# A decoder layer with eight experts: weight chunks rounded first, one tile's products in three parts, scores turned four tiles at a time

## The reference, cut to what matters

```python
x = layernorm(x + attention(x))                     # causal, 16 heads of 128
x = layernorm(x + cross_attention(x, ctx))          # linear attention, gated, 16 heads of 32
x = layernorm(x + ffn(x))

def ffn(h):                                          # h: 896 tokens x 512
    logits = h @ router_weight.T + router_bias       # 8 experts
    top_vals, top_idx = top_k(logits, 2)
    scores = zeros_like(logits).at[rows, top_idx].set(softmax(top_vals))
    gate_up = einsum('th,ehj->etj', h, gate_up_proj) + gate_up_proj_bias
    gate, up = minimum(gate_up[..., ::2], 7), clip(gate_up[..., 1::2], -7, 7)
    act = (up + 1) * gate * sigmoid(1.702 * gate)
    expert_out = einsum('eti,eih->eth', act, down_proj) + down_proj_bias
    return einsum('te,eth->th', scores, expert_out)
```

## Time and profile before

| what | value |
|---|---|
| median of 3 runs | 908.39 us (906.37 to 908.43) |
| the profiled execution | 907.49 us, span 905.7 us |
| PE busy (matmul) | 836.1 us, 92% of the span |
| DVE, ACT, POOL busy | 468.6, 309.7, 103.6 us |
| mean granted clock of PE | 0.964 |
| chain that ended last | PE 71%, no visible wait ("issue") 9%, DVE 8%, ACT 7% |

### The profile page before, as it was taken

The page is one execution under the profiler, slowest core; times in us unless marked ns, Lnnn a source line. Parts: engine busy times, 40 slices in busy tenths (PEclk is TensorE's granted clock), DMA queues, the critical chain, the costliest instruction groups (busy, mean ns, idle before and its releaser), DMA issues.

```text
span 905.7 us, 12521 instructions
## 1 busy us (share of the span) xinstructions
PE 836.1 (92%) x4878; PEld 731.5 (81%) x4878; DVE 468.6 (52%) x867; ACT 309.7 (34%) x705; POOL 103.6 (11%) x95
## 2 busy tenths in 40 slices
PE   7999999999999999899999999999778999999970
PEld 6998997989898989788898788888557787888760
DVE  4445454544536462758622443556756666656424
ACT  4533333232424342532432121222223454444420
POOL 0000000000000000000000001102301323443342
PEclk9999999999999999999999999999859999999995
DMA  9680817240202012022100111102763546654325
GB/s 331 242 280 6 284 38 233 89 160 32 96 1 87 13 25 98 6 85 91 35 1 1 35 35 58 46 13 96 290 201 120 178 144 168 179 132 107 73 35 182
DMA packets 35903, 97.92 MB, mean 108 GB/s; under 512 B 6649, under 2 KB 9081, under 8 KB 33153
## 3 DMA queue, kind: packets, MB, share of 16 engines
q1 hardware_dynamic: 32032, 88.62, 28.5%
q0 software_dynamic: 3808, 8.46, 5.1%
HBM read 64.03 MB, written 32.12 MB: 106 GB/s over the span
## 4 chain that ended last, share of the span: by engine, by line
PE 71%; issue 9%; DVE 8%; ACT 7%; DMA 2%; POOL 2%; POOLq 0%; SPq 0%; ACTq 0%; DVEq 0%
PE bank L306 57%; PE bank L655 3%; ACT w_gu L1031 3%; PE bank L687 2%; PE bank L584 2%; POOL y_acc L511 1%; DVE hh L1833 1%; PE bank L643 1%; DVE prob L1393 1%; DMA y_acc<-y,meta 1%; ACT x_g L1258 1%; PE bank L561 1%; DVE gl L1820 1%; PE bank L725 1%; DVE w_gu L1346 1%
## 5 line engine op out<-in xcount | busy, mean ns | idle before, releaser
L306 PE MATMUL bank<-w_kv,cT 128*125 128x512 f32 x576 | 143.6, 400 | 0.9 <-DVE acc L1380 0.9
L306 PE MATMUL bank<-xT,w_qkv 128*128 128x512 f32 (+1 forms) x672 | 137.9, 365 | 1.9 <-ACT qT L1063 1.9
L306 PEld LDWEIGHTS bank<-xT,w_qkv 128*128 128x128 f32 x672 | 122.0, 188 | 17.2 <-issue 2.0
L306 PE MATMUL bank<-x_g,w_gu 128*128 128x288 f32 x768 | 116.2, 312 | 16.5 <-DVE w_gu L1346 11.3
L306 PEld LDWEIGHTS bank<-x_g,w_gu 128*128 128x128 f32 x768 | 111.1, 202 | 20.1 <-DVE w_gu L1346 14.3
L306 PEld LDWEIGHTS bank<-w_kv,cT 128*125 128x125 f32 x576 | 104.1, 186 | 24.8 <-issue 1.3
L463 POOL TENSOR_TENSOR ln_rs<-ln_ve,half 128x1 f32<-128x1 f32 (+2 forms) x16 | 12.6, 790 | 636.2 <-DVE ln_ve L1475 636.2
L306 PE MATMUL bank<-w_o,zT 128*128 128x512 f32 x336 | 79.8, 395 | 0.5 <-DVE acc L1678 0.5
L306 PE MATMUL bank<-w_qkv,xT 128*128 128x256 f32 x588 | 77.3, 287 | 0.0
L306 PEld LDWEIGHTS bank<-w_o,zT 128*128 128x128 f32 x336 | 61.7, 188 | 15.0 <-DVE acc L1380 1.8
L306 PEld LDWEIGHTS bank<-w_qkv,xT 128*128 128x128 f32 x588 | 72.2, 191 | 0.0
(11 more groups left out here) (152 smaller groups left out, 1184.5 us busy)
## 6 DMA issues: line engine op xcount, KB each, us to landing
x_rows<-blank SPq DMA_DIRECT2D x9, 2084.0 KB, 15.8
raw_gu<-in_w_gu_dram SPq DMA_DIRECT2D x8, 2048.0 KB, 7.7
raw_w<-in_w_qkv_dram SPq DMA_DIRECT2D x22, 512.0 KB, 6.8
raw_dn<-in_w_down_dram SPq DMA_DIRECT2D x8, 1024.0 KB, 4.8
raw_c<-in_ctx_t_dram SPq DMA_DIRECT2D x8, 750.0 KB, 4.4
raw_o<-in_w_o_dram SPq DMA_DIRECT2D x8, 512.0 KB, 3.9
xg<-x_rows SPq DMA_DIRECT2D x8, 512.0 KB, 5.6
raw_kv<-in_w_kv_dram SPq DMA_DIRECT2D x2, 1024.0 KB, 7.0
```

What stands on the lines that cost most here:

```text
L306: last = nc.tensor.matmul(mm_out, lhs(a, k), rhs(b, k), start=(k == 0 and i == 0), stop=(k == n - 1 and i == 2))
```

## The change

- **Experts, ACT and DVE.** From expert 2 on, the weight chunk q of the next expert is rounded first in quarter q (q = 0 to 3), ahead of the sigmoid; on DVE its remainder comes after the hidden part and ahead of the gathered rows and the hidden part's remainder (`splits_at`, `SPLITS`). For expert 1 three chunks are split before expert 0 and the last in its first quarter; for expert 2 one in the last quarter of expert 1 and three at its end. ACT evacuates the down pieces behind the chunks as before, but nothing of the next weights stands between the last quarter and them.
- **Last expert.** PE does all four quarters, then `down(6)`, then `down(7)`; `down_last` is gone. Its down weights are split in its second quarter.
- **Tile 5 in three parts.** `cross_out(5)` is split in 3, 6 and 3 products, around `attended(7)` and `turn_atn(7)`; its sum is added before `a_low(7)`, its statistics after (`cross_stats`).
- **Scores.** `turn_scores(i)` transposes four tiles (then three) into one bank, with one split each; the split scores keep a place for all tiles. `down_bias(0)` moves behind `router(6)`, `rank(5)` and `assign(5)` ahead of `router(6)` and `choose(6)`; the biases of tiles 5 and 6 are added behind the first gather, and POOL scatters tile 4 ahead of tile 6's inverse deviation.
- **Small.** The third piece of the first gather uses bank 0 and waits for nothing; the wait for banks 6 and 7 moves to the end of expert 0.

```diff
-        scoreT = [one(f"scoreT{i}", a, 2 * P).rearrange("p (s c) -> p s c", s=2) for i, a in enumerate((25136, 24112))]
+        scoreT = [one(f"scoreT{i}", 19968 + i * T, T) for i in range(2)]
...
-            last = [("st", 0), ("rk", 4), ("db", 0), ("t1", 5), ("rt", 5), ("t1", 6), ("rt", 6),
...
+            last = [("rk", 4), ("st", 0), ("t1", 5), ("rt", 5), ("t1", 6), ("rk", 5), ("rt", 6), ("db", 0), ("rk", 6),
+                    ("cnt", 0), ("db", 1), ("db", 2), ("st", 1), ("db", 3), ("db", 4), ("db", 5), ("db", 6)]
...
+        HALVES = ((0, 4), (4, NT))
+        SPLITS = {0: ((3,), (), (), (), ()), 1: ((), (), (), (0,), (1, 2, 3))}
+
+        def splits_at(e, q):
+            if e + 1 == NE:
+                return ()
+            return SPLITS[e][q] if e in SPLITS else (q,) if q < KC else ()
+
+        def gather_bank(e, k):
+            return 4 + (3 * e + k) % 2 if e or k < 2 else 0
...
             inverse_std(1, 5, 6, 8)
+            scatter(4)
             inverse_std(1, 6, 7, 9)
-            scatter(4)
...
+            def turn_scores(i):
+                pe.wait_ge(m["score_ok"], HALVES[i][1])
+                o = take(route, "st", i)
+                for n in range(*HALVES[i]):
+                    j = n - HALVES[i][0]
+                    mm = nc.tensor.transpose(o[0:NE, j * P:(j + 1) * P], row[:, n, D:D + NE], ident[:, :])
+                mm.then_inc(ready("st", i)[0], 1)
...
             sums(23)
-            turn_score(0)
+            cross_out(5, 0, 1)
             attended(7)
-            cross_out(5)
+            cross_out(5, 1, 3)
             turn_atn(7)
+            cross_out(5, 3, KC)
             rank(4)
-            down_bias(0)
+            turn_scores(0)
             cross_out(6)
             turn_x2(5)
             router(5)
             turn_x2(6)
+            rank(5)
             router(6)
-            rank(5)
-            turn_score(1)
+            down_bias(0)
             rank(6)
             count()
             down_bias(1)
-            for n in range(2, NT):
-                turn_score(n)
+            down_bias(2)
+            turn_scores(1)
+            for n in range(3, NT):
                 down_bias(n)
...
-                    if e and q == (3 if e + 1 < NE else 1):
-                        for k in range(3):
-                            down(e - 1, k)
-            down_last()
+                if e == 0:
+                    for k in range(6, 8):
+                        pe.wait_ge(free[k], LAST[k])
+                else:
+                    for k in range(3):
+                        down(e - 1, k)
+            for k in range(3):
+                down(NE - 1, k)
...
                 for q in range(KC):
-                    if q == 2 and not more:
-                        for k in range(3):
-                            y_evac(e - 1, k)
-                        dn_high(e, e % 2)
+                    for k in splits_at(e, q):
+                        gu_high(e + 1, (e + 1) % 2, k)
                     swish(e, q)
                     if e == 0 and q:
                         gather_high(1, q - 1)
+                    if q:
+                        h_high(e, q - 1, hT[e % 2])
                     if q >= 2 and e and more:
                         gather_high(e + 1, q - 2)
-                    if q:
-                        h_high(e, q - 1, hT[e % 2])
...
                     clamp(e, q, gu_b[:, e])
...
+                    if q:
+                        hidden(e, q - 1)
+                    for k in splits_at(e, q):
+                        gu_low(e + 1, (e + 1) % 2, k)
                     if q >= 2 and e and more:
                         gather_low(e + 1, q - 2)
                     if q:
-                        hidden(e, q - 1)
                         h_low(e, q - 1, hT[e % 2])
+                    if q == 1 and not more:
+                        dn_low(e, e % 2)
```

More of the change, by code:

```diff
@@ L736, in turn_atn, with cross_out @@
                 mm.then_inc(ready("turn", b)[0], 1)
[L738 to L744 removed]
+            def cross_out(n, k0=0, k1=KC):
+                if k0 == 0:
+                    pe.wait_ge(m["a_lo"], wo_needs(n))
+                    if n == 0:
+                        pe.wait_ge(m["wx_lo"], WX["wxo"])
+                    take(late, "wo", n)
+                for k in range(k0, k1):
+                    for i, (a, b) in enumerate(PASSES):
+                        mm = nc.tensor.matmul(bank("wo", n)[:, :], xT[:, a, k, n * P:(n + 1) * P], w_xo[:, b, k, :],
+                                              start=(k == 0 and i == 0), stop=(k == KC - 1 and i == 2))
+                if k1 == KC:
+                    mm.then_inc(ready("wo", n)[0], 1)
             def turn_x2(n):
@@ L1844, in _ @@
                 for q in range(KC):
-                    if q == 2 and not more:
-                        dn_low(e, e % 2)
                     clamp(e, q, gu_b[:, e])
```

151 lines of the change are left out of this document (57 added, 94 removed).

## The result

| | before | after |
|---|---|---|
| median | 908.41 us (906.37 to 909.62, 4 runs) | 877.55 us (877.32 to 879.96, 4 runs) |
| ratio, 95% interval | | 0.9668 (0.9644 to 0.9693) |
| span of the profiled execution | 905.7 us | 875.5 us |
| mean granted clock of PE | 0.964 | 0.974 |

The kernel is 3.3% faster, 30.9 us by the medians, 30.2 by the spans. To compare traces I cut each at four starts: the first `w_xo` product of the cross attention ("origin"; everything ahead of it is the same program in all kernels), and the first gate/up products of experts 0, 1 and 7.

What follows compares the result with a forecast made beforehand. PE was taken as bounded by waits on gate/up weight remainders and turned scores. Gains 7.4 + 2.9 + 11.0 + 6.0 + 4.0 = 31.3 off 907.49 gave 876.2, by the median 877.1; forecast 876.5 us, range 872 to 886.

Steps and rivals of the forecast that it cites:

- Step 1: Front, sixth tile's products in three parts: the last attention tile starts at 637.8, not 639.99; gain 2.2 us.
- Step 2: Front, routing order: two new waits take back 1.0 us; last scatter near 652.6, not 655.53; rows' load at 656.4.
- Step 3: Front, scores by four tiles: seven round trips become two, gather near 661, first expert at 664.5; gain 7.4 us.
- its own sign of error: Front: the prediction's stated mark that the scores step is wrong, the gather beginning with a wait on DMA; no size.
- Step 4: Expert 0 to 1: PE's idle of 4.51 us shrinks to 1.6, the late last gathered piece; gain 2.9 us.
- Step 5: Experts 2 to 7: with the chunk first on ACT, PE's six waits on weight remainders go; gain 11.0 us.
- The rule against it: Experts: DVE and POOL exclude each other in SBUF; POOL first costs DVE some 0.85 us a quarter, 3.3 in all.
- Step 6: Experts 1, 2, 5 and 7: without stalls they start at full clock, 1.5 us each; gain 6.0 us.
- Step 7: Last expert: the 2.97 us idle before its down products and their slow start go, adds come later; gain 4.0 us.
- The rival of blocked ACT: Experts: ACT waits for the next weights' transfer; slower than before from a landing of 25.0 us on; chance 0.03.

Runs made afterwards that it cites:

- the old order: Kernel after with DVE's quarter, and ACT's gathered rows and hidden part, in the order of before; ACT still rounds the weight chunk first: 875.65 us.
- the late run: Kernel after with the next gate/up weights' transfer asked for only after the down products of the expert before: 909.76 us.
- the run with fillers: Kernel after with 21 more 128x128 products on PE whose results nothing uses, around the last tiles' turns and before the first gather: 877.88 us.

## Why the prediction was right, by its steps

- **Step 1** (sixth tile): 637.8 was foreseen, 637.96 came. The run with the tile whole puts its price at 1.0 us at the seventh tile.
- **Step 2** (routing order): router 6 at 646.3, was 646.20. But I had taken it, the bias behind it and the last rank at full clock; they ran at the lower level, and the last scatter started at 653.50 instead of 652.6. This is the 0.9 that the rows were late; in the two traces whose last router took 1.04 and 1.25 us without fillers, they were asked for 1.1 to 1.2 earlier.
- **Step 3** (scores): the biases ended at 660.0, foreseen 660.3. The gather should have started near 661 with both chains level; the rows came last, after a wait of 2.04. The step's size failed by 1.1 (6.3 against 7.4), and its own sign of error, a gather that begins with a wait on DMA, named the cause.
- **Step 4** (expert 0 to 1): idle 1.77, foreseen 1.6; gain 3.1 against 2.9, of which 0.4 is expert 0's first quarter (4.97 us instead of 5.35), which the step did not count.
- **Step 5** (experts): mechanism and size hold, 15.1 with the clock against 15.5. What the prediction did not separate is which of the moved orders matters: the chunk ahead of the sigmoid on ACT keeps the whole gain by itself. The rest of the new order costs 0.19 us per expert.
- **The rule against it** was real but smaller: DVE lost 0.61 us a quarter instead of 0.85, the third gather started 0.19 late per expert instead of 0.55. With the old order, and so without the meeting, an expert takes 22.55 instead of 22.74. The Trainium skill, "SBUF — State Buffer", section "Who interferes with whom", calls the ports that DVE and GpSimd share an exclusive lock, and names a DVE instruction with two inputs in SBUF beside a GpSimd instruction that reads SBUF as such a case. The trace agrees that the one that comes second is held up (POOL's product at 741.39, the remainder at 741.54), though the remainder lost 0.61 of the 0.75 us in which the two overlap.
- **Step 6** (clock): 6.0 was right in this execution, partly by luck. The wait ahead of expert 1 was called harmless. Ten traces have it, 1.76 to 1.86 us long: in four expert 1 begins at full clock (two quarters in 6.63 or 6.64), in six at the lower level (8.13 to 8.15). By these counts the gain to expect there was 0.6 us, not 1.5.
- **Step 7** (last expert): 6.9 us behind the last product against 7.0; the order is worth 4.1 by itself against 4.0.
- **The rival of blocked ACT** had a chance of 0.03 because the transfer lands in time, and that was right. Its working was not. It let PE stall only from a landing 20.4 us behind the gate/up products, 11.8 into the next expert: 5.3 us that cost nothing, and 6.5 more for the fourth chunk. In the late run's first such expert the weights are there 8.1 us in, 17.6 behind the products, and PE already waits 0.6 and 2.6 us; with landings 8.1 to 11.6 in, 10.1 on average, the kernel is level with before, for which the working wanted 16.4 (25.0 less the 8.6). The term that failed is the 6.5: the 5.3 is close to the 4.9 that the rows of that expert give. I asked when DVE needs ACT's first product, and not what stands behind the first weight remainder on DVE, the gate and up of the second quarter, whose banks PE needs 10.6 us in.

## What to carry to other kernels

Where two engines hand work to each other in turn, the place of an operation matters on the engine that starts the chain: moved forward there it removed 11 us of waits, moved forward on the second engine too it brought nothing and met another engine's operation. A copy of late data at the head of a queue makes that data's transfer critical; before doing it, take the time to the first thing queued behind its consumer, not behind itself. And a stall of some 2 us on PE costs its length and, in 14 of the 20 cases of 1.76 to 2.21 us ahead of an expert in these traces, 1.5 us of slow products after it; the eight of 0.96 to 1.36 us cost only their length.

## What the runs showed of the hardware

- The same wait leaves TensorE's clock at 1.00 or sends it to 0.50: four against six of ten traces, with 1.8 us of idle each. The run with the last expert's old order has the same program as the kernel after up to there, and its two quarters took 8.15 us instead of 6.63. The Trainium skill, "TensorE: Matmul & The Clock Gate", Part 1, says that the window of the monitor behind the clock is free-running and does not reset when a kernel starts, so that the moment of a change depends on where the first product falls in it; that both outcomes occur with one program up to there agrees.

```profile
683.97 8.15 PE L306 MATMUL bank<-x_g,w_gu 128*128 128x288 f32 x48 [1.77 <-DVE x_g L1360]
```

- A PE busy 10.00 of 10 us does not mean the full clock: from 650 to 660 us, with the bias products of 8 rows by 512 columns, the granted clock was 0.50, and in the run with fillers it was 0.50 there too and 0.95 in the ten us behind them. What in the products makes the difference no run here separates.
- The first 515 us, the same program in all fourteen traces, took from 513.3 to 516.0 us, and the load of the gathered rows 4.7 or 6.1 us in two executions of one kernel. Differences of about 1 us between single traces need an origin near the change, and the medians decide.
